# Two opening rounds in a written order, a second home for raw weights, and other PSUM banks for three stages

## Time and profile before

| | us |
|---|---|
| median of 3 runs | 2082.75 (2080.5 to 2086.22) |
| profiled execution, its own time | 2090.85 |
| its span, first to last instruction | 2089.1 |
| first step of round 0 begins | 28.59 |
| first step of round 1 begins | 76.58 |
| first step of round 2 begins | 122.65 |
| one of rounds 2 to 14 | 47.9 |

### The profile page before, as it was taken

How to read it: one execution, slowest core, us unless ns; L and a number is a source line. 1 busy time by engine, 2 the same in 40 slices (tenths; PEclk the granted TensorE clock), 3 DMA queues, 4 the chain that set the end, 5 groups by cost and what they waited for, 6 DMA issues and landing times. The chain is left out here.

```text
span 2089.1 us, 35151 instructions
## 1 busy us (share of the span) xinstructions
PE 1910.4 (91%) x13798; PEld 1624.2 (78%) x13798; DVE 1394.5 (67%) x2817; ACT 803.8 (38%) x1484; POOL 639.8 (31%) x507
## 2 busy tenths in 40 slices
PE   4689999999999999999999997999988988988997
PEld 2368888888888878999999996677676777767886
DVE  5677877787788875655555553588866857783654
ACT  3445445454555542322222221454444443232332
POOL 1333333333333331000000000576755620002563
PEclk9699999999999999999999998999999988998999
DMA  4211212211111115222222222644433444324674
GB/s 120 73 52 66 77 61 73 81 67 67 62 62 62 62 42 181 71 101 101 92 101 101 101 72 89 231 114 141 159 106 122 143 157 143 109 94 142 163 184 64
DMA packets 111750, 214.64 MB, mean 103 GB/s; under 512 B 14242, under 2 KB 34786, under 8 KB 110562
## 3 DMA queue, kind: packets, MB, share of 16 engines
q1 hardware_dynamic: 104194, 195.30, 27.8%
q0 software_dynamic: 7392, 17.11, 4.0%
HBM read 136.11 MB, written 76.34 MB: 102 GB/s over the span
## 5 line engine op out<-in xcount | busy, mean ns | idle before, releaser
L1372 PE MATMUL psum<-kv,toep 128*128 128x288 f32 x1280 | 328.3, 419 | 43.1 <-ACT yx L1420 27.1
L1372 PEld LDWEIGHTS psum<-kv,toep 128*128 128x128 f32 x1280 | 249.3, 196 | 119.5 <-ACT yx L1420 32.7
L168 PE MATMUL psum<-xn_t_h,w_gate_h 128*128 128x256 f32 x768 | 233.2, 304 | 1.3 <-DVE th L292 1.3
L170 PE MATMUL psum<-xn_t_h,w_gate_l 128*128 128x256 f32 x768 | 217.6, 283 | 0.0
L169 PE MATMUL psum<-xn_t_l,w_gate_h 128*128 128x256 f32 x768 | 217.6, 283 | 0.0
L168 PE MATMUL psum<-xn_t_h,w_up_h 128*128 128x256 f32 x768 | 217.5, 283 | 0.0
L169 PE MATMUL psum<-xn_t_l,w_up_h 128*128 128x256 f32 x768 | 217.5, 283 | 0.0
L170 PE MATMUL psum<-xn_t_h,w_up_l 128*128 128x256 f32 x768 | 216.6, 282 | 0.0
L1038 POOL TENSOR_SCALAR_AFFINE_SELECT operands<-operands 128x512 f32<-128x512 f32 x128 | 93.9, 734 | 354.9 <-ACT operands L781 354.9
L275 ACT ACTIVATE th<-psum 128x256 f32<-128x256 f32 x192 | 73.8, 384 | 308.8 <-PE psum L170 308.1
L161 POOL TENSOR_TENSOR rstd<-rstd,minus_half 128x2 f32<-128x2 f32 x48 | 35.0, 730 | 503.6 <-DVE rstd L157 503.6
(11 more groups left out here) (305 smaller groups left out, 4733.9 us busy)
## 6 DMA issues: line engine op xcount, KB each, us to landing
toep<-ssm_padded_scratch SPq DMA_DIRECT2D x64, 256.0 KB, 3.6
kx<-in_ctx_pairs SPq DMA_DIRECT2D x32, 384.0 KB, 4.2
x_scratch<-x_all SPq DMA_DIRECT2D x21, 512.0 KB, 2.8
x_all<-in_x SPq DMA_DIRECT2D x16, 512.0 KB, 3.8
operands<-in_ctx_t SPq DMA_DIRECT2D x16, 512.0 KB, 4.8
xn_t_scratch<-xn_t_h SPq DMA_DIRECT2D x16, 512.0 KB, 2.7
xn_t_scratch<-xn_t_l SPq DMA_DIRECT2D x16, 512.0 KB, 3.6
xn_t_h<-xn_t_scratch SPq DMA_DIRECT2D x16, 512.0 KB, 3.7
```

What stands on the lines that cost most here:

```text
L168: pe.run.matmul(out, lhs[0], rhs[0], start=first, stop=False)
L170: return pe.run.matmul(out, lhs[1], rhs[0], start=False, stop=last)
L1372: ins = pe.run.matmul(out, w[:, (o - k) * P:(o - k + 1) * P], pairs, start=(k == 0), stop=(k == o))
```

## The change

1. `xn2` and the two `th` tiles become one tile of 1536 numbers per partition, which is also a first stage for raw weights; the old stage is the second. Pieces alternate, each stage has its semaphore, and a load waits only for the piece two before.
2. `load_batch` is cut into `load_x` and `load_ctx`, the context has one semaphore per buffer, and the loads have places of their own in the list. The context of batch 0 is issued behind the gate weights and the norm scale.
3. The list for the operands of batch 0 and for rounds 0 and 1 is written out. Batch 1's normalising and turning come before round 0, batch 2's before round 1, the logarithm, decays, parts and rows of the next batch in earlier slots, weights in slots 0, 2, 4 and 8 of round 0 and 1 and 7 of round 1. Rounds 2 and later keep `slots(b)`.
4. Setting up `unfold` moves from `setup_router` to `setup`; `setup_router` moves ahead of `gates_log`.
5. Banks: the second half of down goes to bank 6 in all batches (before: 5, but in the last two); `rows` to bank 5 (before: 6); `norms` to bank 7 except for batch 0 (before: 6); turned queries of batches 1 and 2 to bank 5.

```diff
-            xn2 = sb("xn2", [P, ST, D])
-            th = [sb(f"th{i}", [P, S]) for i in range(2)]
+            xn2_th = sb("xn2_th", [P, ST * D + 2 * S])
+            xn2 = xn2_th[:, 0:ST * D].rearrange("p (t d) -> p t d", t=ST)
+            th = [xn2_th[:, ST * D + i * S:ST * D + (i + 1) * S] for i in range(2)]
...
-                stages = [x_all[:, 3 * XB:3 * XB + RAW]]
+                stages = [xn2_th[:, :], x_all[:, 3 * XB:3 * XB + RAW]]
...
-                c_loaded = signal("c_loaded")
+                c_loaded = [signal(f"c{i}_loaded") for i in range(2)]
...
-                def operands(b):
-                    return [("load", b), ("load_values", b), ("normalise_x", b), ("apply_x", b), ("turn_query", b, 0),
-                            ("turn_query", b, 1), ("setup", b), ("sum_values", b), ("gates", b), ("gates_log", b),
-                            ("decays", b), ("parts", b), ("values", b), ("setup_router", b), ("load_weights", 0), ("weights", 0),
-                            ("load_weights", 1), ("norms", b), ("rows", b)]
+                first_operands = [("load_rest", 0), ("load_values", 0), ("load_x", 1),
+                                  ("load_weights", 0), ("load_ctx", 1), ("load_weights", 1), ("load_x", 2),
+                                  ("normalise_x", 0), ("apply_x", 0), ("turn_query", 0, 0), ("turn_query", 0, 1), ("setup", 0),
+                                  ("sum_values", 0), ("gates", 0), ("setup_router", 0), ("gates_log", 0), ("normalise_x", 1),
+                                  ("apply_x", 1), ("decays", 0), ("parts", 0), ("norms", 0), ("turn_query", 1, 0),
+                                  ("turn_query", 1, 1), ("rows", 0), ("values", 0)]
+                first_slots = [
+                    [("step", 0, 0), ("exp", 0, 0), ("gates", 1), ("load_values", 1), ("store_kernel", 0), ("weights", 0),
+                     ("load_weights", 2)],
+                    [("step", 0, 1), ("exp", 0, 1), ("gates_log", 1)],
+                    [("step", 0, 2), ("exp", 0, 2), ("decays", 1), ("weights", 1), ("load_weights", 3)],
+                    [("step", 0, 3), ("exp", 0, 3), ("weighted", 0, 0), ("parts", 1), ("sum_values", 1)],
+                    [("step", 0, 4), ("exp", 0, 4), ("turn_h", 0, 0), ("rows", 1), ("norms", 1), ("values", 1), ("weights", 2),
+                     ("load_weights", 4)],
+                    [("step", 0, 5), ("exp", 0, 5), ("weighted", 0, 1)],
+                    [("step", 0, 6), ("exp", 0, 6), ("turn_h", 0, 1), ("normalise_x", 2)],
+                    [("step", 0, 7), ("exp", 0, 7), ("weighted", 0, 2), ("apply_x", 2)],
+                    [("step", 0, 8), ("turn_h", 0, 2), ("weights", 3), ("load_weights", 5), ("load_ctx", 2)],
+                    [("weighted", 0, 3)],
+                    [("step", 1, 0), ("exp", 1, 0), ("turn_h", 0, 3), ("sums", 0), ("turn_query", 2, 0)],
+                    [("step", 1, 1), ("exp", 1, 1), ("turn_query", 2, 1), ("spread", 0, 0), ("weights", 4)],
+                    [("step", 1, 2), ("exp", 1, 2), ("spread", 0, 1), ("load_values", 2), ("gates", 2)],
+                    [("step", 1, 3), ("exp", 1, 3), ("weighted", 1, 0), ("residual", 0)],
+                    [("step", 1, 4), ("exp", 1, 4), ("turn_h", 1, 0), ("statistics", 0), ("gates_log", 2)],
+                    [("step", 1, 5), ("exp", 1, 5), ("weighted", 1, 1), ("decays", 2)],
+                    [("step", 1, 6), ("exp", 1, 6), ("normalise", 0), ("turn_h", 1, 1), ("sum_values", 2), ("parts", 2)],
+                    [("step", 1, 7), ("exp", 1, 7), ("turn_x", 0, 0), ("weighted", 1, 2), ("turn_x", 0, 1), ("values", 2),
+                     ("router", 0), ("weights", 5)],
+                    [("step", 1, 8), ("rows", 2), ("norms", 2), ("logits", 0), ("turn_h", 1, 2), ("shares", 0)],
+                    [("weighted", 1, 3)]]
...
-                split_in = {(0, 1): 1, (0, 4): 2, (0, 7): 3, (1, 1): 4, (1, 4): 5}
-                order = operands(0)
-                for b in range(B + 2):
+                order = list(first_operands)
+                for slot in first_slots:
+                    order += slot
+                for b in range(2, B + 2):
...
-                    if name in ("turn_query", "turn_x"):
-                        banks.plan((name, b, at[0]), ((7, 4) if b == B - 1 else (6, 7))[at[0]] if name == "turn_x" else 6)
+                    if name == "turn_query":
+                        banks.plan((name, b, at[0]), 5 if b in (1, 2) else 6)
+                    elif name == "turn_x":
+                        banks.plan((name, b, at[0]), ((7, 4) if b == B - 1 else (6, 7))[at[0]])
                     elif name in ("gates", "norms", "rows"):
-                        banks.plan((name, b), 6)
+                        banks.plan((name, b), {"gates": 6, "norms": 7 if b else 6, "rows": 5}[name])
...
-                        banks.plan((name, b, 0, at[0]), 5 + at[0] * (b >= B - 2))
+                        banks.plan((name, b, 0, at[0]), 5 + at[0])
...
                         elif name == "load_weights":
-                            sp.wait_ge(weight_low, splits_before(b))
+                            if b >= len(stages):
+                                sp.wait_ge(weight_low, splits_before(b - len(stages) + 1))
                             load_weights(0, b, stages, stage_loaded)
```

More of the change, by code:

```diff
@@ L438, in build_program @@
                 x_moved = [signal(f"x{i}_loaded_then_stored") for i in range(4)]
-                c_loaded = signal("c_loaded")
+                c_loaded = [signal(f"c{i}_loaded") for i in range(2)]
                 gate_w_loaded = signal("gate_w_loaded")
                 router_loaded = signal("router_loaded")
-                stage_loaded = [signal("stage_loaded")]
+                stage_loaded = [signal(f"stage{i}_loaded") for i in range(len(stages))]
                 ssm_loaded = signal("ssm_loaded")
@@ L530, in build_program @@
                                 order.append(stage)
[L531 to L535, removed]
                 order += [("weights2", GH + i) for i in range(JH // PER)]
@@ L741, in scalar_attention @@
                         elif name == "weights":
-                            act.wait_ge(stage_loaded[0], loaded_by(b, 1))
+                            act.wait_ge(stage_loaded[b % len(stages)], loaded_by(b, len(stages)))
                             for src, parts_ in pieces[b]:
@@ L1072, in sync_attention @@
                                      ).then_inc(gate_w_loaded, 16)
-                    first = True
+                    load_ctx(0)
                     for name, b, *at in order:
-                        if name == "load":
-                            if b:
-                                load_batch(b)
-                            else:
-                                sp.run.dma_start(dom[:, :], io["dominant"].rearrange("(a n) -> a n", a=1)).then_inc(dom_loaded, 16)
-                                sp.run.dma_start(wr_raw[:, :, :], io["gate_weight_t"].rearrange("(k p) n -> p k n", p=P)
-                                                 ).then_inc(router_loaded, 16)
-                                for c in range(3):
-                                    sp.run.dma_start(merge_i[c * NE:(c + 1) * NE, :], io["merge"].rearrange("(n a) -> n a", a=1)
-                                                     ).then_inc(router_loaded, 16)
-                                sp.run.dma_start(lag0, io["ssm"][:, 0:8]).then_inc(ssm_loaded, 16)
-                                sp.run.dma_start(dskip, io["skip"].rearrange("(n a) -> n a", a=1)).then_inc(ssm_loaded, 16)
-                        elif name == "normalise_x" and b == 1:
+                        if name == "load_x":
+                            load_x(b)
+                        elif name == "load_ctx":
+                            load_ctx(b)
+                        elif name == "load_rest":
+                            sp.run.dma_start(dom[:, :], io["dominant"].rearrange("(a n) -> a n", a=1)).then_inc(dom_loaded, 16)
+                            sp.run.dma_start(wr_raw[:, :, :], io["gate_weight_t"].rearrange("(k p) n -> p k n", p=P)
+                                             ).then_inc(router_loaded, 16)
+                            for c in range(3):
+                                sp.run.dma_start(merge_i[c * NE:(c + 1) * NE, :], io["merge"].rearrange("(n a) -> n a", a=1)
+                                                 ).then_inc(router_loaded, 16)
+                            sp.run.dma_start(lag0, io["ssm"][:, 0:8]).then_inc(ssm_loaded, 16)
+                            sp.run.dma_start(dskip, io["skip"].rearrange("(n a) -> n a", a=1)).then_inc(ssm_loaded, 16)
+                        elif name == "store_kernel":
                             sp.wait_ge(ssm_padded, 1)
```

20 lines of the change are left out of this document (10 added, 10 removed).

## The result

The changed kernel takes 2054.26 us (median of 4 runs, 2047.86 to 2057.9), the kernel before 2084.47 on the same chip (2080.5 to 2086.22): 30.2 us less, ratio 0.9849 [0.9825, 0.9874]. The forecast was 2054. The profiled execution after took 2051.07 us.

What follows compares the result with a forecast made beforehand. Full rounds were taken as bound by TensorE's work plus about 1.4 us of gaps, rounds 0 and 1 by hand-overs between engines. Banks 18 plus opening 11 off 2090.85, less 8.1 for the profiled execution, gave 2054; range 2043 to 2068.

Steps and rivals of the forecast that it cites:

- The banks: End of each full round: norms starts 0.75 us earlier, down's second half 0.58, no wait replacing them; 18 us taken.
- Rival 2: Full rounds: the banks give nothing, another wait stands right behind each; 2072 us, chance 0.07.
- The opening: Rounds 0 and 1: the new order gains 7.2 us by round 0 and 4 in round 1, together 11 us.
- Round 0: Steps laid out at the lower clock level from step 0 at 31.4; round 1 starts at 69.4 against 76.58.
- the middle of two bounds: Round 1: gain between 0 (each removed wait replaced) and 8 us (TensorE stays at the higher level); 4 taken.
- The stalls: Opening rounds: ACT idle 4.27 us for raw weights, TensorE 8.96 before rows; 13.2 us lose their cause.
- What is late next is DVE: Round 0: once the load of weights finds its stage free, the stall at 37.23 has no successor and DVE is late next.
- The added wait: Round 1: the load of context 2 stands behind that of weights 5; gates 2 may wait about 1 us.
- Only moved to the left: After round 15: the work there is only shifted earlier; no gain or loss counted.
- taking 8.1 us off the profiled time: Whole kernel: the profiled execution lay 8.1 us above the median of 2082.75, so 2061.9 became 2053.8.
- Rival 3: Rounds 2 to 15: without the gaps the granted clock falls, 6.5 us per hundredth; 2106 us at 0.92, chance 0.05.

Runs made afterwards that it cites:

- the banks alone: Kernel before with only the three bank moves (second half of down to 6, rows to 5, norms to 7), its own order kept: 2063.49 us, ratio 0.9896.
- context moved: Changed kernel with the load of context 2 issued ahead of the splits of weights 3 and the load of weights 5: 2049.92 us, ratio 0.9829.
- order alone: Changed kernel with the three bank moves undone, the written order and second stage kept: 2072.78 us, ratio 0.9946.
- norms back: Changed kernel with norms back in bank 6, rows in 5 and the second half of down in 6: 2051.58 us, ratio 0.9842.
- two splits later still: Changed kernel, context 2 earlier, splits of pieces 0 and 1 in slots 3 and 5, 2 and 3 in slot 8 and round 1's slot 0: 2051.71 us.

## Why the prediction was right

**The banks.** Right in mechanism and size. 0.75 + 0.58 = 1.33 us a round was predicted and 47.85 - 46.51 = 1.34 measured; norms alone gave 0.77. Rival 2 did not come true. The Trainium skill (page "TensorE: Matmul & The Clock Gate", section "HAM oscillation — how this bites in real kernels") tells of a kernel where PSUM double-buffering gave no further gain; here the banks alone gave 19.9 us, so that case does not carry over to this kernel. What decided was the trace: waits that name a bank's reader as the releaser. Two details of the argument were too loose. The parts were priced one by one, but that nothing takes over the waits is true of the moves together only: with down moved alone, `rows` takes over. And norms' own move was credited with 0.75 us where the move of `rows` would have done it.

**The opening.** The term that was mis-sized, by the trace: 11 us predicted, 14.4 measured. (By the end times the opening is 30.2 - 18.4 = 11.8 us, which the intervals cannot tell from either.) By its parts: step 0 starts 2.4 us later than before (2.8 predicted), round 0 takes 36.0 (38.0, from 31.4 to 69.4), round 1 41.3 (42).

Round 0 was worked out rightly step by step. DVE's multiplications end at 40.5, 43.3, 49.3, 53.7 and 57.9 us, where 41.1, 43.9, 49.5, 53.8 and 58.7 were predicted. Only its end came early, at 66.94 instead of 69.4, and that is mostly the clock: the prediction laid all steps at the lower level, and from 63.9 us on TensorE ran at the higher one, 0.92 us for scores that take 1.65 in the kernel with the context moved. In three kernels where it did not (order alone, norms back, context moved) round 1 starts at 68.79, 68.85 and 69.04; in the kernel with one stage, where it did, at 67.30.

For round 1 the prediction took 4 us as the middle of two bounds, and the order alone gave 3.5; the closeness of that is luck. What was left out are the banks' effect inside rounds 0 and 1, where two waits of `norms` (0.68 and 0.96) also vanish: 1.5 us, shown by the banks alone. The remaining 14.4 - 11.3 - 1.5 = 1.6 us are of the size of what the clock does in these rounds, but no run takes them apart, and why the clock rises at 64 us in one kernel and not in another was not settled.

**The stalls.** The 8.96 us were put down to the chain of batch 1 at the end of round 0. That is about half of it: with the chain put back 4.74 us return. The rest goes by the trace to the splits of piece 3 between logarithm and decays (4.70 us), which the prediction did not name. The 4.27 us of ACT were put down to the single stage: with one stage and the new order the time is the same, and 1.5 us of that wait are left. So the order, which leaves time between splits, is enough to end most of this stall. "What is late next is DVE" held: the longest waits left in round 0 are for L964, and two further ways of placing the splits only moved them.

**The added wait.** Gates 2 wait 3.88 us for the load of context 2, where about 1 was predicted; the sum gave it no price, and taking it away gave nothing, as DVE's multiplication ends there too.

**The rest.** "Only moved to the left" holds for the code after round 15, but a single execution of it varies: from the last copy of turned queries in the second half (L1191, after the change L1219) to the end the same instructions took 796.3 us in the profile before and 789.6 in the one after, and 786.1 to 796.8 over the twelve profiled executions. The two profiled executions differ by 39.8 us (2090.85 and 2051.07) where the medians differ by 30.2. Of the 39.8, 32.0 lie up to the copy of `rows` shown above, 1.1 between the two copies, and 6.7 in this last part. These 6.7 and the 1.5 of the 49.34-us round are 8.2 us of one execution's chance, so taking 8.1 us off the profiled time, as the prediction did, was right here. The two small misses (opening 3.4 too little, a median of before that came out 1.7 higher here) are of opposite sign, so 2054 against 2054.26 is partly luck; 28.7 against 30.2 us of gain is the fair comparison. Rival 3 did not come true: the granted clock is 1.00 over the full round shown above.

## What to carry to other kernels

Where a wait's releaser is the reader of a bank and not the writer of an operand, price it by the time between the end of the matmul ahead and the start that the wait allows; here that came out within 0.02 us a round. Then look what else is in the new bank, because moves of single stages can hand the wait on to the next user, and only the set of moves removes it. Where engines hand work to each other and none is full, look at what stands between a producer and the next consumer on the engine that is late: half of the longest stall was a split of weights between the logarithm and the decays that needed it. Moving a chain that the next round needs to an earlier place gave time; moving splits that stand ahead of some step in any place only moved the wait. Before adding a second buffer for a late load, see whether the order can leave the first one time to be refilled; here it could. And compare openings only between executions whose clock runs alike: the pair with the same clock showed in one row what the pair with different clocks hid.

## What the runs showed of the hardware

The granted clock is 1.00 over a full round in which TensorE is busy 46.31 of 46.50 us. In the opening rounds the level differs between executions of nearly the same list: 1.00 in one and 0.54 in another over the same 8 us. The same 16 matmuls of `gates` take 3.65 us in the full change at 76.16 and 1.93 at 74.64 in the kernel without the wait of 3.88 us ahead of them; the first ran at the lower level, 1.2 GHz, the others at the higher. The idle time ahead does not decide that by itself: in the kernel with norms back they stand behind a wait of 1.90 us and take 1.93 too, and in the kernel with two splits later still they take 3.66 at 76.11 with no wait ahead.

The granted clock of the first rows of a profile is to be read with care. In the kernel before it is given as 1.00 from 28.59 to 53 us and in the earlier trace rows, yet the 16 matmuls of `gates` take 3.66 us at 13.07, as long as those at the lower level. So the 0.83 of round 0 in the earlier trace rows is too high; here the durations are the better sign.

One round of 49.3 us among rounds of 47.85 stood in the kernel before and in the one with the order alone, and in none of the other ten kernels. In both the granted clock fell to the lower level inside that round, the kernel before first:

```profile
507.20:510.60 3.40, 3.40 (x19) 3.40 (x18) 0.78 (x4) 1.94 (x3) 1.88 (x2) 0.50 0.69 203
```

```profile
639.70:643.10 3.40, 3.40 (x19) 3.40 (x18) 0.79 (x4) 1.92 (x3) 1.89 (x2) 0.50 0.71 204
```

Both stretches begin 1.9 us behind a wait of `norms` for the copy of `rows`, and these two are the kernels in which that wait and the one of down stand in every full round. The other rounds with the same waits show no such fall, so that the waits bring it about is not shown.
